# Attention with a quantised linear layer on eight cores: weight loads and casts moved, the rank-16 additions placed one block later, and waits for whole barriers replaced by waits for single users

## The reference

```python
xn = layernorm(x)                                # x: 4 x 4096 x 1024
q, k, v = xn @ Wq.T, xn @ Wk.T, xn @ Wv.T        # 1024 x 1024 each
attn = softmax(causal(q @ k.T / 32)) @ v
s = max(abs(kernel)) / 7                         # over the whole 1024 x 1024 matrix
w = clip(round(kernel / s), -8, 7) * s
out = x + attn + (xn @ w + bias + (xn @ a) @ b)  # a: 1024 x 16, b: 16 x 1024
```

## Time and profile before

| | value |
|---|---|
| profiled execution, span | 1052.65 us, 1051.1 us |
| PE busy, share | 747.6 us, 71% |
| DVE, ACT, POOL | 475.5, 279.1, 39.1 us |
| PE in the chain that ended last | 58% |
| DMA in that chain | 14% |
| DVE in that chain | 11% |

### The profile page before, as it was taken

One profiled execution on the slowest core, in us unless ns is written; L12 is line 12 of the kernel. 1 busy time (PEld: TensorE's weight loads), 2 busy tenths in 40 slices (PEclk: granted clock), 3 DMA queues, 4 the chain that ended last, 5 costly groups with the idle time before them and its releaser, 6 DMA issues.

```text
span 1051.1 us, 12170 instructions; the slowest of 8 cores (1039.9 to 1051.1 us)
## 1 busy us (share of the span) xinstructions
PE 747.6 (71%) x3122; PEld 319.5 (30%) x3184; DVE 475.5 (45%) x792; ACT 279.1 (27%) x623; POOL 39.1 (4%) x68
## 2 busy tenths in 40 slices
PE   0046908879797797941589888566998979888773
PEld 0012302324233342420134333222443434343331
DVE  0027404749466474881642642144714324334434
ACT  1032203232341423311332211003143342433331
POOL 1000000000000000001000000000010010110111
PEclk9986958889897988985789998878999989998996
DMA  8940551032140401017705211587631544414334
GB/s 178 208 138 1 90 56 55 6 96 41 60 100 1 101 1 61 5 55 113 113 41 118 85 79 80 184 277 220 193 103 64 163 121 161 121 43 118 121 121 160
DMA packets 36952, 106.47 MB, mean 101 GB/s; under 512 B 3317, under 2 KB 14840, under 8 KB 32408
## 3 DMA queue, kind: packets, MB, share of 16 engines
q0 software_dynamic: 20640, 40.96, 19.3%
q1 hardware_dynamic: 16248, 64.73, 18.7%
HBM read 92.11 MB, written 29.36 MB: 116 GB/s over the span
## 4 chain that ended last, share of the span: by engine, by line
PE 58%; DMA 14%; DVE 11%; issue 10%; ACT 5%; SPq 1%; DVEq 0%; ACTq 0%; POOL 0%; POOLq 0%
PE psAV L981 13%; PE psS L881 10%; PE psK L421 9%; PE psV L455 7%; PE psQ L665 5%; DMA ab_sb<-wvT 5%; PE psF L696 4%; DMA qtile<-qT_h 2%; DMA scr_h<-gcol 2%; PE T L378 2%; ACT sq L341 1%; PE psT L966 1%; PE T L351 1%; PE T L381 1%; DMA xga<-xcols 1%
## 5 line engine op out<-in xcount | busy, mean ns | idle before, releaser
L981 PE MATMUL psAV<-v_res,ptb 128*128 128x512 bf16 x527 | 148.0, 384 | 22.7 <-ACT ptb L972 11.6
L455 PE MATMUL psV<-wvb,xg 128*128 128x512 bf16 x498 | 121.3, 403 | 1.7 <-issue 1.2
L421 PE MATMUL psK<-xg,wkb 128*128 128x512 bf16 x503 | 116.2, 388 | 0.5
L972 ACT COPY ptb<-psT 128x128 bf16<-128x128 bf16 x272 | 70.7, 267 | 171.2 <-PE psT L966 169.0
L881 PE MATMUL psS<-k_res,qtile 128*128 128x512 bf16 (+1 forms) x236 | 65.5, 442 | 49.7 <-DMA qtile<-qT_h 29.5
L981 PEld LDWEIGHTS psAV<-v_res,ptb 128*128 128x128 bf16 x544 | 51.8, 97 | 91.1 <-issue 70.5
L455 PEld LDWEIGHTS psV<-wvb,xg 128*128 128x128 bf16 x512 | 52.2, 103 | 76.5 <-issue 23.9
L1000 DVE SCALAR_TENSOR_TENSOR outsb<-psAV,invl,fft 128x512 f32<-128x512 f32 x16 | 12.0, 751 | 134.0 <-PE psT L966 72.1
L421 PEld LDWEIGHTS psK<-xg,wkb 128*128 128x128 bf16 x512 | 50.3, 99 | 65.9 <-issue 9.2
L893 DVE CAST scores<-psS 128x512 bf16<-128x512 f32 x72 | 47.5, 660 | 49.7 <-PE psS L881 49.2
L881 PE MATMUL psS<-kbuf,qtile 128*128 128x512 bf16 (+1 forms) x330 | 68.2, 363 | 0.9 <-DMA kbuf<-kT_h 0.6
(11 more groups left out here) (98 smaller groups left out, 805.4 us busy)
## 6 DMA issues: line engine op xcount, KB each, us to landing
kbuf<-kT_h SPq DMA_DIRECT2D x21, 1024.0 KB, 7.5
kT_h<-kst SPq DMA_DIRECT2D x8, 1024.0 KB, 4.2
ff_h<-ffst SPq DMA_DIRECT2D x16, 512.0 KB, 2.8
...
xg<-xfm POOLq DMA_DIRECT2D x7, 1024.0 KB, 8.6
...
```

The source lines that it names most:

```text
L421: P.op("T", lambda e, g=g, dc=dc, cc=cc: e.matmul(psK[dc % 2][:, :], wkb[:, :].rearrange("p (a x) -> p a x", a=NCH)[:, cc, dc * 128:(dc + ...
L455: P.op("T", lambda e, g=g, tt=tt, h=h, cc=cc: e.matmul(psV[tt % 2][h][:, :], xg[g % 3][:, cc * G1 + tt * 128: cc * G1 + (tt + 1) * 128], w ...
L972: ptb_ev[kc] = P.op("S", lambda e, kc=kc: e.copy(out=ptb[kc % 3][:, :], in_=psT_[kc % 2][:, :]), waits=wv, inc=chS)
L981: av_lastk[kc] = P.op("T", lambda e, si=si, kc=kc, h=h, nk=nk: e.matmul(psAV[si % 2][h][:, :], ptb[kc % 3][:, :], v_res[:, kc * C + h * 51 ...
```

## The change

Three groups of edits, shown below without what only serves the allocation of memory.

1. Wv's second half, all casts of Wv (now all four on DVE) and the first six `wker` loads are added after `e_xn(1)` instead of at the start; `e_ab_iter` moves from kproj 1 to kproj 2; the 8 quants are spread over the rounds g = 2 to 7 by a table, with their loads.
2. `bar1` is no longer waited for. Each first use of a reused buffer waits for that buffer's last user (`p1_last`). Wq comes as fp32 in two halves through SP, each half cast by ACT in two instructions; half 0 is issued in kproj 7, half 1 after half 0's casts. The first two loads of stage 2's blocks wait for the slots that they take.
3. In stage 3, `k_res`, the mask and the first four `qtile` loads wait for the buffers' users only; `kbuf`, `fft` and `xrt` still wait for `bar2`.

```diff
-    for h in range(2):
-        wv_Y[h] = P.op("Y", ... wvT half h ..., waits=(wv_cast[0] if h == 1 else []), inc=chY)
-        for q, eng in ((0, "V"), (1, "S")):
+    wv_Y[0] = P.op("Y", ... wvT half 0 ..., inc=chY)
+    def e_wv_tail():
+        for h in range(2):
+            if h == 1:
+                wv_Y[1] = P.op("Y", ... wvT half 1 ..., waits=wv_cast[0], inc=chY)
+            for q in range(2):
+                toks.append(P.op("V", ... tensor_copy ..., waits=[wv_Y[h]], inc=chV))
+        for i in range(6):
+            w = [] if i < 2 else list(wv_cast[1])
+            qa_y[i] = P.op("Y", ... wker row block i ..., waits=w, inc=chY)
...
+    def wq_hook(dc):
+        if dc == NCH - 1:
+            kp7tok[0] = chT.tok()
+            wq_h0_Y[0] = P.op("Y", ... wqT half 0 ..., waits=[kp7tok[0]], inc=chY)
+    quant_sched = {2: [0], 3: [1], 4: [2], 5: [3], 6: [4, 5], 7: [6, 7]}
+    qdma_sched = {3: [2], 4: [3], 5: [4], 6: [5], 7: [6, 7]}
...
     e_bcast(1); e_xn(1)
+    wv_done = e_wv_tail()
     e_kproj(0)
     e_scan()
...
+        for qi in qdma_sched.get(g, []):
+            e_qdma(qi)
         e_vproj(g - 1)
         if g <= NG1 - 1:
-            e_kproj(g, extra=(e_ab_iter if g == 1 else None))
+            ex = e_ab_iter if g == 2 else (wq_hook if g == 7 else None)
+            e_kproj(g, extra=ex)
...
-        if g - 1 < NCH:
-            e_quant(g - 1)
-        if g + 1 < NCH:
-            e_qdma(g + 1)
+        for qi in quant_sched.get(g, []):
+            e_quant(qi)
...
+    for h in range(2):
+        if h == 1:
+            wq_h1 = P.op("Y", ... wqT half 1 ..., waits=[wq_cast[0]], inc=chY)
+        for q in range(2):
+            tk = P.op("S", lambda e, dst=dst, srcv=srcv: e.copy(out=dst, in_=srcv),
+                      waits=[wq_h0_Y[0] if h == 0 else wq_h1,
+                             p1_last["wvb"] if q == 0 else None], inc=chS)
+        wq_cast[h] = tk
...
     def e_stats2(b, bankfree):
             if cc == 0:
-                w += [bankfree, bar1]
+                w.append(bankfree)
...
-    wq_dma = P.op("G", ... wqT, cast to bf16 ..., waits=[bar1], inc=chG)
...
     kres_dma = [
-             waits=[bar2], inc=chY),
+             waits=[wq_cast[1], kst_Y[0]], inc=chY),
...
     def e_sdma_qt(k):
-        w0 = [bar2] if k < 2 else []
+            w0 = [qp3_T, qst_Y[j // 4]] if k < 2 else []
```

More of the change, by code:

```diff
@@ L115, in replay @@
                 ins.then_inc(sems[semname], amt)
+_DBG = {}
 def build_nc():
@@ L245, in build_nc @@
     qa_y = {}
-    for i in range(6):
-        w = [] if i < 2 else list(wv_cast[1])
-        qa_y[i] = P.op("Y", lambda e, i=i: e.dma_start(
-            out=scan_buf(i), in_=d["wker"][i * 128:(i + 1) * 128, :]),
-            waits=w, inc=chY)
     qmax_done = {}
@@ L557, in build_nc @@
     xntmp2_b = sb2("xntmp2_b", [128, G1], F32)
+    sqa = [sb2(f"sqa{i}", [128, G1], BF16) for i in range(2)]
     xnt2 = [xntmp2, xntmp2_b]
@@ L584, in e_stats2 @@
             wsq = [xga_dma[b]]
+            if b == 0 and cc <= 1:
+                wsq.append(p1_last["sqb"])
             key = (b, cc - 2) if cc >= 2 else (b - 1, cc + 6)
@@ L600, in e_stats2 @@
                 start=(cc == 0), stop=(cc == NCH - 1), skip_group_check=True),
-                waits=[sq2_S[(b, cc)]], inc=chT)
+                waits=[sq2_S[(b, cc)]] + ([bankfree] if b == 0 and cc == 0 else []),
+                inc=chT)
         stats2_T[b] = chT.tok()
     def e_math2(b, prev=()):
+        reg = [p1_last["kst_even"]] if b == 0 else []
         v0 = P.op("V", lambda e: e.tensor_copy(out=s1a, in_=U0[0:1, :]),
-                  waits=[stats2_T[b]] + list(prev), inc=chV)
-        v1 = P.op("V", lambda e: e.tensor_copy(out=s2a, in_=U1[0:1, :]), inc=chV)
+                  waits=[stats2_T[b]] + list(prev) + reg, inc=chV)
+        v1 = P.op("V", lambda e: e.tensor_copy(out=s2a, in_=U1[0:1, :]),
+                  waits=reg, inc=chV)
         v2 = P.op("V", lambda e: e.tensor_tensor(
@@ L630, in e_xn2 @@
     def e_xn2(b):
+        reg = [p1_last["kst_odd"]] if b == 0 else []
         P.op("V", lambda e: e.tensor_copy(out=mbc2[:, :], in_=U0[:, :]),
-             waits=[bcast2_T[b]], inc=chV)
+             waits=[bcast2_T[b]] + reg, inc=chV)
         ev = P.op("V", lambda e: e.tensor_copy(out=rbc2[:, :], in_=U1[:, :]),
-                  inc=chV)
+                  waits=reg, inc=chV)
         bcastev2_V[b] = ev
@@ L667, in e_qproj @@
                     wqb[:, :].rearrange("p (a x) -> p a x", a=NCH)[:, cc, dc * 128:(dc + 1) * 128],
-                    xga[b % 3][:, cc * G1:(cc + 1) * G1],
+                    xga[SL[b]][:, cc * G1:(cc + 1) * G1],
                     start=(cc == 0), stop=(cc == NCH - 1)), waits=w, inc=chT)
             tmm = chT.tok()
+            wse = [tmm] + ([qst_S[b - 2]] if dc == 0 and b >= 2 else [])
+            if b <= 1 and dc == 0:
+                wse.append(p1_last["strow"] if b == 0 else p1_last["xnrow"])
             ev[dc] = P.op("S", lambda e, b=b, dc=dc: e.activation(
@@ L675, in e_qproj @@
                 func=AF.Copy, scale=SCALE),
-                waits=[tmm] + ([qst_S[b - 2]] if dc == 0 and b >= 2 else []), inc=chS)
+                waits=wse, inc=chS)
         qst_S[b] = ev[NCH - 1]
@@ L718, in e_ffn @@
         ff_V[b] = evs[3]
+    e_xga(1)
     e_xga(0)
-    e_xga(1)
-    wq_dma = P.op("G", lambda e: e.dma_start(
-        out=wqb[:, :].rearrange("p (a x) -> p a x", a=NCH),
-        in_=d["wqT"].rearrange("(a p) x -> p a x", p=128)), waits=[bar1], inc=chG)
-    e_stats2(0, None); e_math2(0); e_bcast2(0); e_xn2(0)
+    e_stats2(0, p1_last["psT01"]); e_math2(0); e_bcast2(0); e_xn2(0)
     e_stats2(1, bcastev2_V[0]); e_math2(1, prev=[math2_V[0], math2_S[0]])
@@ L746, in sb3 @@
     def sb3(n, s, t):
-        return p2b.enter_context(nc.sbuf_tensor(n, s, t))
+        return _rec(n, "p2b", lambda: p2b.enter_context(nc.sbuf_tensor(n, s, t)))
     def ps3(n, s, t=F32):
         return p2b.enter_context(nc.psum_tensor(n, s, t))
+    k_res = sb3("k_res", [128, 2 * NCH * 512], BF16)
+    qtile = [sb3(f"qtile{i}", [128, NCH * 128], BF16) for i in range(4)]
+    maskt = sb3("maskt_s", [128, 256], F32)
     scores = [[sb3(f"scores{p}_{i}", [128, 4096], BF16) for i in range(2)]
@@ L755, in build_nc @@
     kbuf = [sb3(f"kbuf{i}", [128, NCH * 512], BF16) for i in range(KRING)]
-    k_res = sb3("k_res", [128, 2 * NCH * 512], BF16)
-    qtile = [sb3(f"qtile{i}", [128, NCH * 128], BF16) for i in range(4)]
     fftile = [sb3(f"fft{i}", [128, C], F32) for i in range(3)]
@@ L786, in build_nc @@
     mxcols = [sb3(f"mxcols{i}", [128, 8], F32) for i in range(2)]
+    assert _rng("k_res") == _rng("wq32")
+    assert _rng("qtile0")[0] == _rng("wqb")[0] and _rng("maskt_s")[1] <= _rng("wqb")[1]
     kres_dma = [
         P.op("Y", lambda e: e.dma_start(out=k_res[:, 0:NCH * 512], in_=kT_h[0, :, :]),
-             waits=[bar2], inc=chY),
+             waits=[wq_cast[1], kst_Y[0]], inc=chY),
         P.op("Y", lambda e: e.dma_start(out=k_res[:, NCH * 512:], in_=kT_h[1, :, :]),
-             inc=chY)]
+             waits=[kst_Y[1]], inc=chY)]
+    t_mk = P.op("Y", lambda e: e.dma_start(out=maskt[:, :], in_=d["maskt"][:, :]),
+                waits=[qp3_T], inc=chY)
     def pump_k(upto):
@@ L978, in em_av @@
                 w2 = [ptb_ev[kc]]
+                if kc == 0 and h == 0 and si == 0:
+                    w2.append(ffev[4 * NB2 - 1])
                 if kc == 0 and h == 0 and si >= 2:
```

133 lines of the change are left out of this document (96 added, 37 removed).

## The result

The changed kernel takes 1009.44 us (median of 10 runs, 1007.47 to 1056.07) beside 1050.79 us for the kernel before in the same comparison (10 runs, 1049.41 to 1053.5). The ratio is 0.9604 with an interval of 0.9589 to 0.9619. So it is about 4% faster. I had forecast 993 with a range of 978 to 1009: the direction was right, the gain was put 16 us too high, and the result lies just outside the range. In some executions the cores of a die show a lower granted clock through long stretches and take longer; the ratios leave those out.

The account below looks back on a forecast made before the run. PE was taken to set the time except in four holes: the start, the scan and the two barriers. Terms -51.0 - 1.0 - 0 - 4.7 = -56.7 took 1052.65 to 995.9, less 3.1 gives 992.9 us; range 978 to 1009.

Parts of the forecast that it names:

- correction of the base: Whole kernel: 3.1 us taken off 995.9, because the median before lay that much below the profiled 1052.65 us.
- fourth term: Second barrier: `k_res` issued 3.3 us earlier, taken as -3.5, and the second `qtile` pair 1.2 earlier; -4.7 us.
- First term: Start to vproj 2: squares no longer wait behind Wv's casts, and the wait at the scan's additions vanishes; -51.0 us.
- rival C: Scan's readback: `scr_h` lands within 12 us, so PE and not DVE sets bcast 2; 983.3 us, chance 0.22.
- Second term: First barrier: it goes, but ACT's four casts of Wq take its place ahead of stage 2's first broadcast; -1.0 us.
- a queue served first: First barrier: if SP's queue were served first, Wq's half 0 would land about 3 us earlier and the term be -4.
- Third term: Stage 2: each `e_stats2` drops its wait on the semaphore list, worth nothing as PE's next stop is DVE; 0 us.
- Rival B: Loads of Wv's half 1 and both Wq halves take 15.4 us each, as beside other traffic; 1006.8 us, chance 0.22.
- D: First barrier: Wq's halves through ACT's list cost over 40 us each, making the kernel slower; 1057.6 us, chance 0.03.
- E: Somewhere not found, a replaced wait holds an engine and eats 15 to 40 us; about 1020 us, chance 0.05.

Follow-up runs that it names:

- e3b: Changed kernel with ACT's casts of Wq, Wq's second-half load and the bias load moved behind stage 2's first sums; ratio 0.9597 to the kernel before.
- e2: Changed kernel with the first barrier's semaphore list waited for again by the first sums of stage 2's blocks 1 to 3; ratio 0.9566 to the kernel before.
- e9: Changed kernel with Wv's first half cast behind xn 0, Wq's first half loaded before quant 7's load, and e2's list waits; ratio 0.9426 to the kernel before.
- e8: Changed kernel with the two `qtile` loads moved directly behind the first half of `k_res` in SP's queue; ratio 0.9525 to the kernel before.
- e4: Changed kernel with the second barrier's list put back in front of `k_res`, the mask and `qtile`; ratio 0.9626 to the kernel before.
- e1: Kernel before with only the first group of edits (Wv, scan, quants), old barriers kept; ratio 0.9729 to the kernel before.

## Why the prediction was right and wrong

The profiled executions differ by 45.8 us where I had summed 56.7, so 10.9 of the 16.5 us are in the sum. The largest misses are the correction of the base (5.6), the fourth term (2.9), the second (2.0) and the third, which I had set to nothing (1.4). By the means over the cores (47.5 us), the terms stand so:

**First term, -51.0: right.** At bcast 7 the cores are 49.8 us earlier; 52.9 at vproj 2 on the two slowest cores. Its inner steps held within 3.4 us: kproj 0 at 62.2 (forecast 59.9, a mean of 59.5 and 60.4 where the later of the two counts; block 1 landed after 41.7 instead of 40.3), PE's pause of 10.75 ended by DVE's casts and vproj 0 at 88.65 (85.3), `scr_h` at 104.83 (104.7), no wait at the additions. Two things were off. Wv's half took 10.18 us, not 9.0. The estimate of 7.9 us from the Trainium skill's "DMA: Bandwidth & Descriptors" (Specifications, and "Anatomy of one DMA") holds on the even cores, where this load took 7.5 to 7.9 us, and not on the odd ones, 10.2 to 10.5. And bcast 2 was ended by PE's own sums, not by DVE, which was through with the scan 1.9 us before it could use them on this core; on core 1, with the write `scr_h` landing 22 us after its issue, DVE ended it at 140.4. The forecast's mechanism and rival C's were both there, on different cores.

**Second term, -1.0: right in mechanism, 2.0 too good in size.** The cores lost 1.0, inside the 1.9 by which this stretch varies. ACT's four casts set the broadcast, with DVE free 8.8 us before the sums were there, as the forecast said and e3b showed by moving the casts behind the squares. The term that was mis-sized is Wq's first half: 17.39 us instead of 14.3 on core 3, issued at the moment forecast, and 12.9 to 17.4 over the cores (mean 15.7). On three cores it took over 16 us, which the prediction had named as a sign that it is wrong. The Trainium skill's rule that each DMA engine alternates between queues ("DMA: Bandwidth & Descriptors", "Queues, rings and completion order") has as its opposite a queue served first, which I had put 3 us below the forecast; core 3 lies 3 above it, so nothing here speaks for SP's queue being served first.

**Third term, 0: failed.** I wrote of the list waits that taking them away "is worth nothing: PE's next stop is DVE". DVE is the next stop, and that is just why it costs: PE arrives earlier, stands for DVE's pieces, and goes on at 1.2 GHz. The eight cores lost 1.4 us, core 3 4.3 against core 2 of before, and 5.9 once the broadcast is earlier (155.7 against 149.8). A row of before had the sign of it, the 1.19 us that PE was already early; I read it as slack; e2 and e9 show that with the list waits the pieces behind run at the higher clock. The Trainium skill's page "TensorE: Matmul & The Clock Gate" ("HAM oscillation") tells of the same loss, a clock that falls when PE waits between bursts of matmuls; the trace agrees (0.50 at 473 to 479 us behind pauses, 1.00 with the list), and I had not weighed it here.

**Fourth term, -4.7: too good by 2.9.** `k_res` was issued 3.1 us earlier behind the last psF (3.3 forecast), but I took that for the gain. `qtile` decides, it stands last in SP's list behind 2 MB of `k_res` and now the mask, and took 17.01 us on the slowest core (13.6 before). 1.2 us came out up to the scores, which is inside the 3.4 us by which this stretch varies, and 0.6 from there to the first transpose, where I had 1.2 for the second pair. e8 shows what the order in the queue is worth, 5.6; the waits' part stays unclear (2.8 by e4, nothing by e1).

**Behind the scores** the changed kernel needs 1.7 us more (297.1 against 295.4 from the first transpose to its end). I had nothing for it. It is not the first group of edits, since e1 has 295.0, and not the second barrier's list on SP's queue, since e4 has 297.5; no run settles the cause. The mean granted clock of the stretch is 0.923 against 0.927 (0.928 in e1), and the single pauses differ by less than 1.5 us each.

These make 1.2 + 2.0 + 1.4 + 2.9 + 1.7 = 9.2 us. Another 1.7 is the slowest core, 7.15 us above the mean of eight instead of 5.47; over nine runs of the changed kernel it is 6.8 to 14.4 and 9.4 on average, 7.5 for the kernel before (27 runs). The last 5.6 come from the base: I took off 3.1 because the profile of before lay that much above the median, and the profile of the changed kernel lies 2.6 below its own, so there was nothing to take off. An early or late landing of `scr_h` on one core of eight could be enough for that, which is not shown.

Rival B's price (15.4 us for each half) was reached by one of three loads (17.39, beside 10.18 and 9.31); it named 1006.8 and was nearest, but not by its mechanism. D and E did not happen. The range ended too early for a plain reason: the bounds I had written for the second term (+6.5) and for the loads were in it, but none for the terms that I had set to nothing, for the slowest core or for the base.
